# Attention and mixture of experts in one kernel: the attention's output projection in three 16-bit passes, and what is reordered around it

## The chip, the cores and the metric

The kernel runs on one core of a Trainium2 chip. The metric is the device time of one execution in microseconds (us). A core has TensorE (PE, with its own queue of weight loads, PEld), VectorE (DVE), ScalarE (ACT), GpSimd (POOL) and SyncE (SP), which here issues the transfers. Each engine runs its own list of instructions in order; they meet at semaphores.

## What is computed

x has 2048 tokens of 512 features. The first half is a recurrence over tokens, in 8 heads of 64, with a decay that depends on the data:

```
xn = layernorm(x) * gamma + beta
w  = sigmoid(xn @ Wx @ Ww + bw);  k = xn @ Wk;  v = xn @ Wv;  r = sigmoid(xn @ Wr)
state = (1 - w_t)[..., None] * state + k_t[..., None] * v_t[..., None, :]     (for each token t)
y_t   = r_t . state
x1 = layernorm(x + y @ Wo)
```

The second half is a mixture of 12 experts, two for each token, and another layernorm. The change touches only the first half. What matters is the product y @ Wo, in f32, for each group of 128 tokens.

## The kernel before, in words

**Chunks and pairs.** The 2048 tokens are 16 chunks of 128 (n = 0 to 15). Two chunks are a pair, and the projections of a pair (decay z, key k, receptance r, value v) are ten jobs on TensorE: jobs 0 and 1 transpose the normalised x (function `job`, L248), 2 and 3 make the decays, 4 and 5 the keys, 6 and 7 the receptances, 8 and 9 the values. They write the two banks of pA in turn, and ScalarE empties them (`take`, L590). The weights of these jobs are held as a high and a low f16 half, and x as xh and xl, so that each product is three f16 matmuls: high by high, high by low, low by high. xh is ScalarE's copy (L620), xl the rest, which VectorE subtracts (`low_x`, L814).

**A chunk on TensorE** (`chunk`, L369) is a list written by hand. scores(0) and scores(1) are the decayed products of keys and receptances for two halves of the heads (pS); between them VectorE copies what the masks select from pS to ST (`mask`, L818, eight instructions). apply_values(0) and (1) multiply ST by the values into pY. read_state adds what the state before gives, turn_keys transposes the decayed keys into pM, from where ScalarE copies them to kbT (L685). write_state makes the state's increment from kbT. attend_out(n − 1) (L341) is the output projection of the chunk before: yT, ScalarE's copy of pY (L724), by w_o, into pM. VectorE adds pM to x (`add_out`, L883) and takes statistics (`take_stats`).

While it does chunk n, TensorE also does jobs of the next pair. `fill(0)` to `fill(4)` are the five places for them. An odd chunk (FIRST) does jobs 0 and 1 and then 2, 3, 4, 5, one in each of the first four places; an even chunk (SECOND) does 6, 7, 8, 9. Chunk 0 is peeled, chunks 1 to 12 are three rounds of a hardware loop of four chunks, so that there are two turns back to the loop's start (after chunks 4 and 8), and chunks 13 to 15 are written out; in these the five places hold the gate's transposes and products, and ScalarE normalises finished tiles (`norms`).

**The levels.** The scores of chunk n + 1 need keys and receptances that are multiplied by products of decays, in seven levels, in the tiles L. VectorE does one half of the receptance levels (`dve_level`, L540, L546, L547, L555), ScalarE copies the other (L502), GpSimd does the keys' half (`pool_level`, L571) and ScalarE copies the rest (L515). The products of decays, AM, are VectorE's `dve_decays` (L525, seven instructions for a pair), at the start of an odd chunk. Besides this ScalarE and GpSimd split the experts' weights into f16 halves, three pieces a chunk (`act_piece` L523, `pool_piece` L577), which SyncE loads and stores.

**Order around the change.** The code sets all of it. TensorE, odd chunk: scores(0), read_state, turn_keys, jobs 0 and 1, projection, job 2, apply(0), scores(1), job 3, write_state, jobs 4 and 5, apply(1). ScalarE, odd chunk: normalise, key level 0, receptance level 1, key level 1, kbT, key level 2, takes 0 and 1, xh, key level 3, the state's decay, key level 4, receptance 2, key 5, receptance 3, a piece, receptance 4, take 2, receptance 5, a piece, take 3 and so on, and yT at the end. VectorE, odd chunk: decays, level 0, mask of scores(0), xl, levels 1 and 2, add_out, levels 3 to 6, mask of scores(1), state, statistics.

## Time and profile before

| What | Value |
|---|---|
| Three runs | 856.07, 857.55, 864.34 us; median 857.55 |
| The profiled execution, its own time | 859.21 us |
| Its span | 857.4 us |
| Mean granted clock of TensorE | 0.932 of full |
| Busy: PE, PEld, DVE, ACT, POOL | 725.9, 525.2, 498.7, 342.1, 328.7 us |

The attention half takes the span from 0 to about 500 us; its loop of chunks runs from about 89 to 410. The rest is the experts. Rows below name an instruction by its line (L349), its engine and operation, what it writes and reads, and how many were merged ("x8"). An f32 matmul is recorded as two. A bracket at the end is the idle time of the engine ahead of the row and what ended it.

### The profile page before, as it was taken

Reading aid. Unit: us, or ns where it says so; the run is one execution under the profiler, and the core shown is the slowest. Engines: PE = TensorE matmul, PEld = TensorE weight load, DVE = VectorE, ACT = ScalarE, POOL = GpSimd, SP = SyncE. Lnnn points to the kernel's source line nnn. Section 1 sums busy time; section 2 is a strip of 40 time slices with the busy share of each in tenths; the row PEclk is TensorE's granted clock in tenths of the full one; section 3 lists DMA queues with packets and bytes.
Section 4 is the critical chain, followed back from the end, with each engine's and each line's share of the span. In section 5 each row is a group of like instructions: output and inputs, shape, how many; then the busy total and the mean of one; then the engine's idle time right before and its main releaser. Section 6 shows DMA issues by size and latency. Waiting matters only on the chain. (4 is left out here: it accounts for less than half of the span.)

```text
span 857.4 us, 18313 instructions
## 1 busy us (share of the span) xinstructions
PE 725.9 (85%) x6030; PEld 525.2 (61%) x6031; DVE 498.7 (58%) x1035; ACT 342.1 (40%) x675; POOL 328.7 (38%) x355
## 2 busy tenths in 40 slices
PE   5879999998999989999969861799999999999400
PEld 2658787876877769778636521466666666666200
DVE  4655867666677646775756558244445444444285
ACT  4454645546345444554466220222222222222154
POOL 0345534542445425454244002243343434333262
PEclk9999999998999989999969975799999999999855
DMA  8615345431454324433342066144466557322394
GB/s 339 225 37 165 117 127 149 148 106 45 149 148 133 105 62 149 141 106 99 101 148 78 22 224 266 50 158 143 165 217 234 197 183 245 122 95 89 134 336 155
DMA packets 38867, 126.75 MB, mean 148 GB/s; under 512 B 3984, under 2 KB 4368, under 8 KB 36496
## 3 DMA queue, kind: packets, MB, share of 16 engines
q1 hardware_dynamic: 31920, 103.31, 35.7%
q0 software_dynamic: 6880, 22.55, 7.7%
q8 instruction: 42, 0.69, 0.3%
q14 instruction: 25, 0.20, 0.1%
HBM read 81.02 MB, written 44.83 MB: 147 GB/s over the span
## 5 line engine op out<-in xcount | busy, mean ns | idle before, releaser
L831 DVE COPY_PREDICATED ST<-msk,pS 128x256 f32<-128x256 uint8 x224 | 121.1, 569 | 100.1 <-issue 65.9
L577 POOL TENSOR_TENSOR piece_parts<-piece,piece_parts 128x1024 f16<-128x1024 f32 x48 | 104.6, 2179 | 115.5 <-ACT piece_parts L523 115.5
L571 POOL TENSOR_TENSOR L<-L,AM 128x256 f32<-128x256 f32 x96 | 70.9, 738 | 118.4 <-ACT L L515 108.8
L1236 PE MATMUL pH<-ring,xgh 128*128 x344 | 104.5, 304 | 5.3 <-issue 2.8
L1237 PE MATMUL pH<-ring,xgh 128*128 x344 | 104.1, 303 | 0.0
L1238 PE MATMUL pH<-ring,xgl 128*128 x344 | 104.1, 303 | 0.0
L299 PE MATMUL pS<-L 64*128 64x64 f32 x1536 | 99.2, 276 | 1.8 <-issue 1.7
L1552 POOL DMA_INDIRECT y_scratch<-ysb,sidx x43 | 42.9, 998 | 136.3 <-DVE ysb L1478 136.3
L299 PEld LDWEIGHTS pS<-L 64*128 64x128 f32 x1536 | 93.6, 192 | 2.1 <-issue 2.1
L1462 DVE TENSOR_TENSOR hid<-pH,sil 128x320 f32<-128x320 f32 x43 | 21.1, 492 | 119.6 <-ACT sil L1315 119.6
L555 DVE TENSOR_TENSOR L<-L,AM 128x256 f32<-128x256 f32 x96 | 70.6, 735 | 16.1 <-ACT L L502 10.0
L1315 ACT ACTIVATE sil<-pH 128x320 f32<-128x320 f32 x43 | 18.8, 437 | 131.0 <-PE pH L1238 131.0
L349 PE MATMUL pM<-w_o,yT 128*128 128x512 f32 x128 | 59.8, 611 | 4.3 <-ACT yT L724 2.8
L523 ACT CAST piece_parts<-piece 128x1024 f16<-128x1024 f32 x48 | 50.1, 1043 | 24.4 <-DMA piece<-in_w_experts 24.4
L1539 POOL DMA_INDIRECT xg<-x_scratch,gidx x43 | 42.7, 994 | 34.0 <-POOL gidx L1536 30.8
L1254 PE MATMUL pO<-ring,hTh 128*128 x129 | 49.0, 380 | 1.8 <-DVE hTh L1473 1.4
L1255 PE MATMUL pO<-ring,hTh 128*128 x129 | 48.9, 379 | 0.0
L1236 PEld LDWEIGHTS pH<-ring,xgh 128*128 128x128 f16 x344 | 34.0, 99 | 24.3 <-issue 11.1
L502 ACT COPY L<-L 128x256 f32<-128x256 f32 x80 | 32.5, 407 | 38.2 <-DVE L L555 26.9
L1311 ACT CAST hTh<-pHT 128x384 f16<-128x384 f32 x43 | 20.6, 479 | 63.9 <-PE pHT L1244 63.9
L1478 DVE COPY ysb<-pO 128x512 f32<-128x512 f32 x43 | 29.7, 692 | 23.0 <-PE pO L1255 23.0
L1237 PEld LDWEIGHTS pH<-ring,xgh 128*128 128x128 f16 x344 | 33.9, 99 | 13.4
(206 smaller groups left out, 1623.6 us busy)
## 6 DMA issues: line engine op xcount, KB each, us to landing
piece<-in_w_experts SPq DMA_DIRECT2D x48, 512.0 KB, 5.5
w_split_scratch<-piece_parts SPq DMA_DIRECT2D x48, 512.0 KB, 3.9
ring<-w_split_scratch SPq DMA_DIRECT2D x12, 2048.0 KB, 8.6
yin<-y_scratch SPq DMA_DIRECT2D x16, 512.0 KB, 5.8
x_scratch<-X SPq DMA_DIRECT2D x1, 4096.0 KB, 14.1
out_x<-X SPq DMA_DIRECT2D x8, 512.0 KB, 2.8
X<-in_x SPq DMA_DIRECT2D x1, 3072.0 KB, 23.3
X<-in_x SPq DMA_DIRECT2D x2, 512.0 KB, 7.5
```

The source lines that it names most:

```text
L299: i = pe.matmul(o, k_, r_, start=True, stop=True)
L349: i = pe.matmul(pM[:, 0, :], yT[:, g, :], w_o[:, g, :], start=(g == 0), stop=(g == KT - 1))
L523: a.copy(piece_parts[buf][:, 0, :], piece[buf][:, :]).then_inc(piece_hi, 1)
L555: v.tensor_tensor(next_grown(k, lv, 1), grown(rec, k, lv, 1), factor(c, lv, 0), ALU.mult).then_inc(r_dec, 1)
L571: g.tensor_tensor(next_kept(k, lv, 0), kept(key, k, lv, 0), by, ALU.mult).then_inc(k_dec, 1)
L577: g.tensor_tensor(piece_parts[buf][:, 1, :], piece[buf][:, :], piece_parts[buf][:, 0, :], ALU.subtract).then_inc(piece_lo, 1)
L831: v.copy_predicated(out[:, :, :, 0 if lv == 0 else 1, :], msk[:, lv, :, :].rearrange(shape, m=m), pS[:, :, lv * S:(lv + 1) * S].rearrange( ...
L1236: pe.matmul(p[:, 0, 0:F], xgh[par][:, k, :], wh, start=(k == 0), stop=False)
L1237: pe.matmul(p[:, 0, 0:F], xgh[par][:, k, :], wl, start=False, stop=False)
L1238: t = pe.matmul(p[:, 0, 0:F], xgl[par][:, k, :], wh, start=False, stop=(k == KT - 1))
L1254: pe.matmul(pO[:, 0, :], hTh[:, k, :], wh, start=(k == 0), stop=False)
L1255: t = pe.matmul(pO[:, 0, :], hTh[:, k, :], wl, start=False, stop=(k == FT - 1))
```

## The change

Wo is held as two f16 halves, wo_h and wo_l, and y as yTh (ScalarE's f16 copy of pY) and yTl (VectorE's subtraction, `low_y`). The projection is three f16 matmuls for each of the four blocks in place of one f32 matmul. Wo arrives in two transfers, in tiles that the second pair doesn't use yet (val[1] and rec[1]); before chunk 0 ScalarE makes wo_h in two copies, and GpSimd makes wo_l in two subtractions between its chunks 0 and 1. ScalarE's takes of jobs 6 and 8 of pair 1 wait until these tiles are read.

The order changes too. On TensorE, apply(1) goes ahead of the place `fill(3)`. In odd chunks jobs 0 and 1 go ahead of read_state, and job 2 goes from ahead of apply(0) to behind scores(1). read_state and the projection wait for y_low as well. On ScalarE, yTh is made behind `fill(2)`; in odd chunks the takes of jobs 0 and 1 go ahead of kbT, and xh and key level 2 follow it. On VectorE low_y comes ahead of level 0, the decays of a pair are made at the end of the even chunk, ahead of the loop's branch, and wait for the decay jobs only.

```diff
-        w_o = sb("w_o", [P, KT, C])
+        wo_h = sb("wo_h", [P, KT, C], F16)
+        wo_l = sb("wo_l", [P, KT, C], F16)
...
+        wo_stage = [val[1][:, :, :], rec[1][:, :, :]]
...
-            sp.dma_start(w_o[:, :, :], wo).then_inc(w_in[5], 16)
+            for i in range(2):
+                sp.dma_start(wo_stage[i], wo[:, 2 * i:2 * i + 2, :]).then_inc(w_in[5], 16)
...
                 pe.wait_ge(y_out, n + 1)
+                pe.wait_ge(y_low, n + 1)
...
             def attend_out(n):
+                pe.wait_ge(wo_lo, 2)
                 pe.wait_ge(y_out, n + 2)
+                pe.wait_ge(y_low, n + 2)
...
                 for g in range(KT):
-                    i = pe.matmul(pM[:, 0, :], yT[:, g, :], w_o[:, g, :], start=(g == 0), stop=(g == KT - 1))
+                    pe.matmul(pM[:, 0, :], yTh[:, g, :], wo_h[:, g, :], start=(g == 0), stop=False)
+                    pe.matmul(pM[:, 0, :], yTh[:, g, :], wo_l[:, g, :], start=False, stop=False)
+                    i = pe.matmul(pM[:, 0, :], yTl[:, g, :], wo_h[:, g, :], start=False, stop=(g == KT - 1))
...
                 scores(n, k, 0)
-                read_state(n, k)
-                turn_keys(n, k)
                 if slots is FIRST:
                     job(q, 0, par)
                     job(q, 1, par)
-                else:
+                read_state(n, k)
+                turn_keys(n, k)
+                if slots is not FIRST:
                     fill(0)
...
+                apply_values(n, k, 0)
+                scores(n, k, 1)
                 if slots is FIRST:
                     fill(0)
-                apply_values(n, k, 0)
-                scores(n, k, 1)
                 fill(1)
                 write_state(n, k)
                 fill(2)
+                apply_values(n, k, 1)
                 fill(3)
-                apply_values(n, k, 1)
                 fill(4)
...
-                    v.wait_ge(a_out, q * JOBS + 8)
+                    v.wait_ge(a_out, q * JOBS + (8 if isinstance(q, int) and q == 0 else 4))
...
             if lv == 0:
+                v.wait_ge(a_out, q * JOBS + 8)
...
+                if isinstance(q, int) and q == 1 and (m == 6 or m == 8):
+                    a.wait_ge(wo_lo, 2)
...
-                if m == 1:
-                    a.wait_ge(a_out, order(q, m) + 1)
-                    a.copy(xh[par][:, :, :], xf[:, :, :]).then_inc(x_hi, 1)
+            def high_x(q, par):
+
+                a.wait_ge(a_out, order(q, 1) + 1)
+                a.copy(xh[par][:, :, :], xf[:, :, :]).then_inc(x_hi, 1)
...
-                a.wait_ge(m_full, n * 3 + 1)
-                a.copy(kbT[:, :], pM[:, 0, :]).then_inc(kb_out, 1)
-                key_levels(2)
                 if slots is FIRST:
                     take(q, 0, par)
                     take(q, 1, par)
-                key_levels(3)
+                a.wait_ge(m_full, n * 3 + 1)
+                a.copy(kbT[:, :], pM[:, 0, :]).then_inc(kb_out, 1)
+                if slots is FIRST:
+                    high_x(q, par)
+                key_levels(2, 3)
...
                 fill(2)
+                a.wait_ge(st_used, n * 2 + 4)
+                a.copy(yTh[:, :, :], pY[:, 0, :].rearrange("p (g t) -> p g t", g=KT)).then_inc(y_out, 1)
                 norms(2)
                 fill(3)
                 norms(3)
-                a.wait_ge(st_used, n * 2 + 4)
-                a.copy(yT[:, :, :], pY[:, 0, :].rearrange("p (g t) -> p g t", g=KT)).then_inc(y_out, 1)
...
             a.wait_ge(stat1, 9)
+            for i in range(2):
+                a.wait_ge(w_in[5], 32)
+                a.copy(wo_h[:, 2 * i:2 * i + 2, :], wo_stage[i]).then_inc(wo_hi, 1)
             chunk(0, 0, 0, 0, (1, 1, SECOND))
...
-                if k % 2 and nxt is not None:
-                    dve_decays(v, n + 1, nxt, in_pair(k + 1)[0])
+                if not isinstance(n, int) or n:
+                    low_y(n - 1)
                 level(0)
...
                     take_stats(n - 1)
+                if k % 2 == 0 and (not isinstance(n, int) or n == 0):
+                    dve_decays(v, n + 2, nxt + 1, in_pair(k + 2)[0])
+
+            def low_y(n):
+
+                v.wait_ge(y_out, n + 2)
+                v.tensor_tensor(yTl[:, :, :], pY[:, 0, :].rearrange("p (g t) -> p g t", g=KT), yTh[:, :, :], ALU.subtract).then_inc(y_low, 1)
...
-            for n in range(2):
-                pool_chunk(g, n, n, 0)
+            pool_chunk(g, 0, 0, 0)
+            for i in range(2):
+                g.wait_ge(wo_hi, i + 1)
+                g.tensor_tensor(wo_l[:, 2 * i:2 * i + 2, :], wo_stage[i], wo_h[:, 2 * i:2 * i + 2, :], ALU.subtract).then_inc(wo_lo, 1)
+            pool_chunk(g, 1, 1, 0)
```

What this does to the lists, at three places. The line numbers of the changed kernel differ from those of the one before. First TensorE in the first odd chunk of the loop, from the end of scores(0); ISA and REGISTER_ALU are waits and counts. Before:

```order
L299 MATMUL pS<-L 128x64 x12
L304 REGISTER_ALU
L306 REGISTER_ALU
L309 MATMUL pY<-L,state 128x128 x4
L329 MATMUL pM<-idt,L 128x128 x4
L253 ISA
L256 ISA
L259 MATMUL pA<-idt,pair_x 128x128 x8
L349 MATMUL pM<-w_o,yT 128x512 x4
L253 REGISTER_ALU
L263 REGISTER_ALU
```

In the changed kernel:

```order
L306 MATMUL pS<-L 128x64 x12
L260 ISA
L263 ISA
L266 MATMUL pA<-idt,pair_x 128x128 x8
L311 REGISTER_ALU
L314 REGISTER_ALU
L317 MATMUL pY<-L,state 128x128 x4
L337 MATMUL pM<-idt,L 128x128 x4
L359 MATMUL pM<-wo_h,yTh 128x512
L360 MATMUL pM<-wo_l,yTh 128x512
L361 MATMUL pM<-wo_h,yTl 128x512
```

The jobs 0 and 1 (pA<-idt,pair_x) have moved ahead of read_state (pY<-L,state) and turn_keys (pM<-idt,L), which the projection now follows directly, in three f16 passes; behind it job 2 (L270, pA<-xh,wh_z) no longer stands.

Second ScalarE in the same chunk, from key level 1 on (L515 before, L526 after). Before:

```order
L515 COPY L<-L 128x128x2
L684 ISA
L685 COPY kbT<-pM 128x512
L507 REGISTER_ALU
L508 REGISTER_ALU
L515 COPY L<-L 128x64x4
L593 ISA
L601 ACTIVATE pair_x<-pA,vecs 128x256 x2
L593 REGISTER_ALU
L601 ACTIVATE pair_x<-pA,vecs 128x256 x2
L620 CAST xh<-pair_x 128x1024
```

In the changed kernel:

```order
L526 COPY L<-L 128x128x2
L605 ISA
L615 ACTIVATE pair_x<-pA,vecs 128x256 x2
L605 REGISTER_ALU
L615 ACTIVATE pair_x<-pA,vecs 128x256 x2
L703 ISA
L704 COPY kbT<-pM 128x512
L636 CAST xh<-pair_x 128x1024
L518 REGISTER_ALU
L519 REGISTER_ALU
L526 COPY L<-L 128x64x4
```

kbT has gone behind the two takes (pair_x<-pA,vecs), and the copy xh follows it, ahead of key level 2.

Third VectorE at the loop's turn, from the state on. Before:

```order
L867 ISA
L872 TENSOR_TENSOR state<-pM,sdec 64x4x64 x2
L880 ISA
L880 BN_STATS stats<-X 128x6
L936 REGISTER_ALU
L936 COMPARE_AND_BRANCH
L538 TENSOR_TENSOR AM<-dec 128x512
L538 TENSOR_TENSOR AM<-AM 128x256
```

In the changed kernel, from the decays' last products on:

```order
L546 REGISTER_ALU
L549 TENSOR_TENSOR AM<-AM 128x16
L546 REGISTER_ALU
L549 TENSOR_TENSOR dec_end<-AM 128x8
L967 REGISTER_ALU
L967 COMPARE_AND_BRANCH
L906 TENSOR_TENSOR yTl<-pY,yTh 128x512
L558 TENSOR_TENSOR L<-rec,dec 128x256
L559 TENSOR_TENSOR L<-rec,AM 128x256
```

The products of decays (AM<-AM) stand behind the branch before and ahead of it now, and low_y (yTl) is the first instruction behind it.

## Rows read from the trace of the kernel before

**Rows 1.** The page's 40 slices: TensorE busy, granted clock, in tenths.
```profile
PE   5879999998999989999969861799999999999400
...
PEclk9999999998999989999969975799999999999855
```

**Rows 2.** Waits of TensorE, 60 to 430 us: total, times, longest in us.
```profile
PE pA L270 <- DVE xl L816: 4.5, 6, 0.8
...
PE pS L299 <- ACT L L515: 2.9, 1, 2.9
```

**Rows 3.** TensorE's timeline, odd chunk: start, us, engine, line, operation, count, [idle before].
```profile
250.77 0.44 PE L299 MATMUL pS<-rec,key 64*128 64x64 f32 x4
...
254.49 1.16 PE L309 MATMUL pY<-L,state 128*128 128x128 f32 x8
...
256.85 3.67 PE L349 MATMUL pM<-w_o,yT 128*128 128x512 f32 x8
261.33 0.27 PE L270 MATMUL pA<-xh,wh_z 128*128 128x256 f16 x1 [0.81 <-DVE xl L816]
...
270.98 1.06 PE L337 MATMUL pM<-val,kbT 128*128 128x128 f32 x8
...
277.21 0.66 PE L319 MATMUL pY<-ST,val 128*64 128x128 f32 x8
```

**Rows 4.** Timeline of TensorE, chunk 13: projection and the instruction behind it.
```profile
419.27 3.67 PE L349 MATMUL pM<-w_o,yT 128*128 128x512 f32 x8 [0.77 <-ACT kbT L685]
422.87 0.66 PE L319 MATMUL pY<-ST,val 128*64 128x128 f32 x8
```

**Rows 5.** Timeline of TensorE, values job: first and thirteenth matmul.
```profile
407.33 0.38 PE L276 MATMUL pA<-wh_v,xh 128*128 128x512 f16 x1
...
409.92 0.38 PE L276 MATMUL pA<-wh_v,xh 128*128 128x512 f16 x1
```

**Rows 6.** Timeline of VectorE, the odd chunk of rows 3.
```profile
247.98 1.68 DVE L538 TENSOR_TENSOR AM<-dec 128x512 f32<-128x512 f32 x1
...
251.80 0.43 DVE L546 TENSOR_TENSOR L<-rec,dec 128x256 f32<-128x256 f32 x1
...
264.37 2.92 DVE L555 TENSOR_TENSOR L<-L,AM 128x256 f32<-128x256 f32 x2 [0.38 <-ACT L L502]
268.57 1.31 DVE L831 COPY_PREDICATED ST<-msk,pS 128x256 f32<-128x256 uint8 x2 [1.28 <-PE pS L299]
...
273.13 0.42 DVE L834 COPY ST<-pS 64x256 f32<-64x256 f32 x1
```

**Rows 7.** The same form on VectorE (L910): ns, min/median/max.
```profile
L910 DVE TENSOR_TENSOR wl_z<-pS,wh_z x4: 676/688/692, 18.0 to 28.3; 128x512 f16<-128x512 f32 x4
```

**Rows 8.** Timeline of ScalarE, the same odd chunk.
```profile
264.97 0.40 ACT L502 COPY L<-L 128x256 f32<-128x256 f32 x1
```

**Rows 9.** Timeline of GpSimd, the last piece ahead of its chunk 1.
```profile
67.07 2.14 POOL L577 TENSOR_TENSOR piece_parts<-piece,piece_parts 128x1024 f16<-128x1024 f32 x1 [2.63 <-ACT piece_parts L523]
```

**Rows 10.** Timeline of ScalarE, chunk 0.
```profile
71.79 0.59 ACT L685 COPY kbT<-pM 128x512 f32<-128x512 f32 x1 [1.32 <-PE pM L329]
```

**Rows 11.** Timeline of VectorE, chunk 0.
```profile
80.85 2.17 DVE L831 COPY_PREDICATED ST<-msk,pS 128x256 f32<-128x256 uint8 x3
```

**Rows 12.** Timeline of TensorE, chunk 0: apply(0) and apply(1).
```profile
75.40 0.66 PE L319 MATMUL pY<-ST,val 128*64 128x128 f32 x8 [1.03 <-DVE ST L834]
...
88.51 0.66 PE L319 MATMUL pY<-ST,val 128*64 128x128 f32 x8
```

**Rows 13.** Timeline of TensorE, end of the last chunk.
```profile
488.36 0.66 PE L319 MATMUL pY<-ST,val 128*64 128x128 f32 x8
491.85 5.24 PE L349 MATMUL pM<-w_o,yT 128*128 128x512 f32 x8 [2.83 <-ACT yT L724]
```

**Rows 14.** TensorE behind turn 2: length, busy, clock (1.00: 2.4 GHz), DMA.
```profile
306.00:314.00 8.00, 7.91 (x74) 0.58 0.11 39
```

**Rows 15.** Timeline of VectorE, the second loop turn.
```profile
305.23 0.69 DVE L538 TENSOR_TENSOR AM<-dec 128x512 f32<-128x512 f32 x1 [5.14 <-issue]
```

More of the change, by code:

```diff
@@ L116, in attention @@
         kbT = sb("kbT", [P, C])
-        yT = sb("yT", [P, KT, P])
+        yTh = sb("yTh", [P, KT, P], F16)
+        yTl = sb("yTl", [P, KT, P], F16)
         state = sb("state", [P, KT, P])
@@ L166, in attention @@
         y_out = sem("y_out")
+        y_low = sem("y_low")
+        wo_hi = sem("wo_hi")
+        wo_lo = sem("wo_lo")
         m_full = sem("m_full")
@@ L424, in _ @@
             pe.wait_ge(setup_done, 1)
-            pe.wait_ge(w_in[5], 16)
             chunk(0, 0, (1, 1, SECOND))
@@ L751, in _ @@
             take(0, 1, 0)
+            high_x(0, 0)
             high(0)
@@ L763, in _ @@
                 take(q, m, q)
+                if m == 1:
+                    high_x(q, q)
                 if at == 1:
@@ L894, in _ @@
             v.sem_inc(state_new, 1)
+            v.sem_inc(y_low, 1)
             v.sem_inc(x1_ready, 1)
@@ L942, in _ @@
                 chunk(n, n, None if n == NT - 1 else NPAIR - 1)
+            low_y(NT - 1)
             add_out(NT - 1)
```

## The prediction

> **What bounds the kernel now.** I read three views in this order: the page's slices, the waits, and then the timeline engine by engine over one odd and one even chunk. The slices show that TensorE is nearly full from about 60 to 410 us, and that after the loop (slice 20 and later) it is not [rows 1]. The waits of that stretch say the same from the other side: TensorE waits little there, 4.5 us for the low half of x (six times, once per odd chunk) and 2.9 us at one loop turn [rows 2]. So in the twelve looped chunks every microsecond of matmul counts, as long as VectorE delivers its masks in time. In the last three chunks and at the end other waits decide.
>
> The timeline of the odd chunk that starts at 250.77 is my measure [rows 3]: scores(0) to 254.49, then read_state, turn_keys and the two transposing jobs to 256.85, the output projection to about 260.45, a wait of 0.81 for the low half of x, job 2 from 261.33, apply(0) and scores(1), write_state at 270.98, apply(1) at 277.21. The next chunk starts at 277.8, so the odd chunk takes 27.0 us.
>
> **The change part by part.**
>
> *Projection in 16 bits.* Before: four f32 matmuls of 512 columns, from 419.27 to the next instruction at 422.87, 3.60 us [rows 4]. Now: twelve f16 matmuls of the same 512 columns. The trace has just that form in the values job: twelve of them start between 407.33 and 409.92, 2.59 us [rows 5]. The gain is 1.0 us for each projection at full clock.
>
> *Even chunks (six in the loop).* Nothing else on TensorE's path changes there but the place of apply(1), which now stands ahead of the last job. In the odd chunk shown the mask of scores(1) runs from 268.57 to 273.55 (273.13 + 0.42) [rows 6] while TensorE, without its last job of 2.65, would ask for it at 277.21 − 2.65 = 274.56 [rows 3]. An even chunk has the same jobs in these places (two jobs and write_state behind scores(1)), so some 1 us is left over. 6 × 1.0 = 6.0 us gained. The bounds are 0 (the mask becomes late by as much) and 6.0.
>
> *New VectorE work.* low_y is a subtraction of a 128x512 f16 copy from PSUM; the trace has that form, 688 ns [rows 7]. It stands ahead of level 0 and so ahead of the mask of the next scores(0). Before an odd chunk VectorE does the decays first: 247.98 to 251.87, 3.9 us [rows 6], then now 0.7 of low_y, then level 0 with some 0.8 to 1.4. That ends near 253.8 against the end of scores(0) at 254.49 [rows 3]: hidden, with 0.7 us to spare. If the cover went, each odd chunk would pay 0.7 or more. The waits for yTh ahead of it (ACT copies it right behind apply(1)) are covered by the last job and scores(0), 2.65 + 3.7 us. Moving the decays to the end of the even chunk changes their place only against the loop's branch and low_y.
>
> *Odd chunks: two waits change places.* The x matmuls of job 2 no longer follow the projection but scores(1), so the wait of 0.8 for the low half goes [rows 2, 3]. But the transposing jobs, which stood between turn_keys and the projection, now stand ahead of read_state, so that nothing covers the copy kbT. Chunk 13 has that order in the trace already: the projection waits 0.77 for kbT [rows 4]; with the latency I count 0.9. One wait pays for the other. Left is the 1.0 of the projection: TensorE would be at the end of job 2 at about 267.3.
>
> *Odd chunks: a new wait behind job 2.* ACT's list is unchanged there: the take of job 2 (L612) stands between the receptance copies of level 4 and level 5. Before, job 2 ended near 264.05 (261.33 and its 2.7) and, behind the take, the level 5 copy ran from 264.97 to 265.37, 1.3 us behind the job's end [rows 8]. Now job 2 ends at 267.3, so that copy ends at 268.6. VectorE's last level waits for it (level 6, the second in the row at 264.37 [rows 6], some 0.5), and only then the mask of scores(1) starts: 269.2. The mask takes 273.55 − 268.57 = 4.98 and ends at 274.2. TensorE meanwhile has done job 3, write_state and job 4 in the 6.2 us between 270.98 and 277.21 shifted [rows 3], 267.3 + 2.65 + 0.9 + 2.65 = 273.5, and wants apply(1): it waits 0.7. So the odd chunk ends at 274.2 + 0.6 + 2.65 = 277.5 instead of 277.8: 0.3 gained, 6 × 0.3 = 1.8 us. Bounds: 1.0 each if the mask is not late (6.0), and 0.5 lost each if it is 1.5 late instead of 0.7.
>
> *Chunk 0.* Wo must be split. ACT copies two 128x1024 pieces, and GpSimd subtracts two, between its chunks 0 and 1. The subtraction has the form of the expert pieces, 2.14 us for the one at 67.07, behind which chunk 1's first key level started at about 69.2 [rows 9]. Two of them push that level to about 73.5, 4.3 us later. ACT's level 1 key copy waits for it and kbT is queued behind. ACT had 1.32 us of idle time ahead of kbT [rows 10], so kbT comes 3.0 later; the levels that follow have about 0.6 of slack more. The mask of scores(1), at 80.85 before [rows 11], starts near 83.2 and ends near 88.2, while TensorE, which had apply(1) behind a last job at 88.51 [rows 12], now wants it at about 85.9. I charge 2.3 us. Bounds: 0 (the slack is larger) and 4.3 (all of it shows). The clock may add to it (below).
>
> *The last three chunks.* TensorE is no longer the bound there [rows 1]: ACT's normalising, VectorE's masks and the gate are. Full gain would be 3.0, none 0, and yTh now stands ahead of some of ACT's normalising and can push gate work by half a microsecond. I take 0.7.
>
> *The last projection.* Before, ACT normalised three tiles and then copied yT: apply(1) at 488.36, projection at 491.85 after an idle 2.83, and 5.24 long because the clock fell in that idle time [rows 13]. Now yTh follows apply(1) at once: 488.36 + 0.6 + 0.6, low_y 0.7 and a hop give 490.3; the twelve matmuls take 5.24 × 2.59 / 3.60 = 3.8. End 494.1 instead of 497.1: 3.0 gained. Bounds 1.5 (same start, less work) and 4.2 (full clock).
>
> Sum: 6.0 + 1.8 − 2.3 + 0.7 + 3.0 = 9.2 us. The experts' part is not touched. The profiled execution took 859.2 (span 857.4), so it would take 850.0; the median shown is 857.55, and 9.2 less is 848.3. A change of 1% (8.6 us) is about what a measurement can tell from no change; the forecast lies just beyond it.
>
> **The clock.** Behind the loop turn at which TensorE had waited 2.9 us, the granted clock was 0.58 in the mean of the 8 us from 306 to 314 [rows 2, 14]: mostly the lower level, 1.2 GHz. That costs a full TensorE 8 × 0.42 = 3.4 us. It did not fall behind the wait of 1.03 in chunk 0 [rows 12] nor behind the 0.8s. The new wait of 2.3 lies between these cases.
>
> **The rivals.**
>
> 1. *The mask is not late in the odd chunks* (0.22). For it: all my terms there are tenths, and VectorE has idle time ahead of that mask (1.28 [rows 6]). Against it: ACT's list. Gain 4.2 more: 844.1.
>
> 2. *The clock falls in chunk 0* (0.20). For it: a wait of 2.3 us. Against: the wait of 1.03 had no such effect. 3.4 more: 851.7.
>
> 3. *VectorE comes late as well at loop turns or at level 0* (0.09). VectorE has a gap of 5.14 us at a turn [rows 15]. It lay ahead of the decays; it will lie between the decays and low_y, for which read_state now waits: the decays to 303.9, a gap of 5.1, low_y 0.7 and level 0 0.8 end at 310.5, against scores(0), which in the slow clock ended near 311.8. Hidden by 1.3 us by these rows; where it is not, or where level 0 meets GpSimd in the other odd chunks, a microsecond for each odd chunk gives 854.5.
>
> The Trainium skill (Runtime: NRT & Kernel Launch, section on instruction fetch mechanics) says that a taken branch to code that isn't in the engine's small window of instructions stops the engine until that page is fetched. By that rule the gap belongs to the branch and not to the decays, so it moves with the branch and can't be hidden by moving the decays; the trace agrees so far as there is such a gap at the turn.
>
> 4. *Slower: the clock falls in every odd chunk* (0.07). Mechanism: each odd chunk now has two waits, 0.9 ahead of the projection and 0.7 ahead of apply(1), in place of one. If these together are enough to bring the clock to half, each costs 3.4 us: 848.3 + 6 × 3.4 = 868.7. [...]
>
> 5. *The gain doesn't show* (0.06): the masks, not the matmuls, set the pace in even chunks too, so only the end gains: 857.55 − 3.0 + 2.3 = 856.9.
>
> The forecast itself has 0.36.
>
> **How the numbers follow.** Time: that of the forecast, 848.3. Faster by over 1% means under 849.0: rival 1 whole (0.22), about six tenths of the forecast's own spread (0.22), and 0.04 for the clock staying up at a turn or at the end: 0.48. Slower by over 1% means above 866.1: rival 4 and a little for what I don't see, 0.08. Within 1%: the rest, 0.44. The range goes from 841 (rival 1 with a better end and one turn without a fall of the clock) to 857 (rival 5), which leaves out rival 4 and thin ends.
>
> **What would show it.** Right: twelve projection matmuls in 2.6 us; TensorE's waits hold kbT ahead of the projection six times with 0.8 to 0.9, VectorE's last copy of ST ahead of apply(1) about six times with 0.7, once with 2.3 in chunk 0, and no wait for xl; the last projection starts within 2.2 us of apply(1). Wrong: a mask of scores(1) in an odd chunk that starts as soon as scores(1) ends (rival 1); a granted clock of 0.50 at about 90 us (rival 2) or in each odd chunk (rival 4); waits of read_state for yTl (rival 3); even chunks that don't shrink from their old length by 1.0 (rival 5).

## The result

The changed kernel took 854.68 us (median of 20 executions, 849.57 to 861.52) against 859.97 of before in the same session (20, 853.37 to 864.34): a ratio of 0.9945, with a 95% interval of 0.9918 to 0.9971. So it is faster by about 0.55%, 4.7 us, where 9.2 us was forecast. (The 4.7 goes by the ratio; the two medians alone lie 5.3 apart.) Two later series of the same kernel, which stand below, gave 0.9922 and 0.9931.

The profiled execution took 860.72 us (span 858.9), which is near the upper end. Against [rows 1] the granted clock lost a tenth in slices 10 and 38 and two in slice 23, and gained one in slice 24; busy time lost one in slices 5, 10, 20 and 22 and gained one in slice 23. A tenth of a slice is only 2 us, so these rows show where to look and not how much.

```profile
PE   5879899997999989999868961799999999999400
...
PEclk9999999997999989999969785799999999999755
```

TensorE's waits from 60 to 430 us, the answer to [rows 2] (total, times, longest in us):

```profile
PE pY L327 <- DVE ST L857: 6.0, 8, 2.3
PE pM L359 <- ACT kbT L704: 5.6, 7, 0.8
PE pS L306 <- issue: 3.5, 2, 2.0
PE pS L306 <- ACT L L526: 2.7, 1, 2.7
```

The wait for xl is gone. kbT stands in its place (0.77 to 0.82 in each odd chunk of the loop, forecast 0.9), the mask ahead of apply(1) is new (0.43 to 0.45 in each, forecast 0.7), and chunk 0 waits 2.29 (forecast 2.3). Here are those three in TensorE's timeline, with the projection of an odd chunk between: from its first matmul at 151.81 to apply(0) at 154.49 it takes 2.68, against 3.60 before [rows 4].

```profile
88.98 0.66 PE L327 MATMUL pY<-ST,val 128*64 128x128 f32 x8 [2.29 <-DVE ST L857]
...
151.81 0.38 PE L359 MATMUL pM<-wo_h,yTh 128*128 128x512 f16 x1 [0.82 <-ACT kbT L704]
...
154.49 0.66 PE L327 MATMUL pY<-ST,val 128*64 128x128 f32 x8
...
168.16 0.66 PE L327 MATMUL pY<-ST,val 128*64 128x128 f32 x8 [0.43 <-DVE ST L857]
```

**Where the time went.** I lay the two profiled executions beside each other by the starts of apply(0). The table's forecast is the sum's own.

| Stretch | Measured, us | Forecast, us |
|---|---|---|
| to apply(0) of chunk 0 (75.40, now 76.10) | +0.7 | 0 |
| chunk 0 with chunk 1 (52.02, now 54.95) | +2.9 | +1.0 |
| three pairs without a turn (52.02, now 50.90, 50.88 and 50.89) | −3.4 | −3.9 |
| pair with turn 1 (57.65, now 58.09) | +0.4 | −1.3 |
| pair with turn 2 (58.38, now 56.91) | −1.5 | −1.3 |
| the last three chunks (12 to 13, 13 to 14, 14 to 15) | −0.6, +1.4, +5.7 | −0.7 |
| the end, up to the experts' first matmul | −3.7 | −3.0 |
| sum, up to the experts (500.48, now 502.50) | +2.0 | −9.2 |

The experts' part is as long as it was (356.9, now 356.4). The one large entry is 14 to 15: 22.48 before, 28.21 now. TensorE's timeline there:

```profile
466.84 0.66 PE L327 MATMUL pY<-ST,val 128*64 128x128 f32 x8 [0.62 <-DVE ST L857]
467.43 0.66 PE L374 MATMUL pA<-idt,X 128*128 128x128 f32 x4
469.30 1.09 PE L374 MATMUL pA<-idt,X 128*128 128x128 f32 x4 [1.21 <-ACT logitT L660]
470.31 0.69 PE L306 MATMUL pS<-rec,key 64*128 64x64 f32 x4
470.80 0.63 PE L306 MATMUL pS<-rec,L 64*128 64x64 f32 x4
471.23 2.77 PE L306 MATMUL pS<-L 64*128 64x64 f32 x24
```

The waits are small, 0.62 and 1.21. But the 24 score matmuls behind them take 2.77 where such a row takes 1.50 at full clock, and L374 with four matmuls takes 1.09 instead of 0.66. The clock was at its lower level, 1.2 GHz, from about 468 to 484, which costs 6.8 us (from the granted clock in steps of 2 us). Two stretches as windows (length, then busy time and count of PE, PEld, DVE, ACT and POOL, granted clock, DMA share, GB/s), chunk 0 and this one:

```profile
86.00:95.00 9.00, 6.71 (x42) 3.03 (x41) 8.10 (x16) 2.96 (x5) 3.58 (x4) 0.81 0.63 191
...
455.00:485.00 30.00, 28.02 (x218) 20.47 (x216) 16.79 (x31) 12.76 (x26) 8.10 (x6) 0.77 0.24 72
```

So the waits are where they were forecast, and near the forecast in size; the clock behind them is not in the forecast's sum. What of this belongs to the change and what to one execution is what the first and the last run ask.

### The profile page after: what moved, and what is told of

It reads as the page before. It is cut to its first block and busy times, and to the rows that moved or that the text cites. A ratio compares the mean times of both kernels' runs of the same rounds, so it can differ in the third digit from the quotient of the medians.

```text
span 858.9 us, 18498 instructions
## 1 busy us (share of the span) xinstructions
PE 720.7 (84%) x6094; PEld 524.8 (61%) x6095; DVE 506.8 (59%) x1051; ACT 344.7 (40%) x677; POOL 334.3 (39%) x357
## 5 line engine op out<-in xcount | busy, mean ns | idle before, releaser
L583 POOL TENSOR_TENSOR L<-L,AM 128x256 f32<-128x256 f32 x96 | 73.6, 767 | 120.4 <-ACT L L526 114.7
L306 PE MATMUL pS<-L 64*128 64x64 f32 x1536 | 102.3, 281 | 2.0 <-issue 2.0
L306 PEld LDWEIGHTS pS<-L 64*128 64x128 f32 x1536 | 96.8, 198 | 2.3 <-issue 2.2
L1273 PEld LDWEIGHTS pH<-ring,xgl 128*128 128x128 f16 x344 | 34.0, 99 | 12.0
```

The source lines that it names most:

```text
L306: i = pe.matmul(o, k_, r_, start=True, stop=True)
L583: g.tensor_tensor(next_kept(k, lv, 0), kept(key, k, lv, 0), by, ALU.mult).then_inc(k_dec, 1)
L1273: t = pe.matmul(p[:, 0, 0:F], xgl[par][:, k, :], wh, start=False, stop=(k == KT - 1))
```

## The experiments

The runs came in three series on three chips, with before in each. The first (before at 858.52 us, 15 executions) has the same kernel again, the three passes, kbT's cover and Wo. The second (858.64, 28) has the order alone, job 2's take, the tail and all four edits. The third (858.42, 16) has the last three runs. Ratios are to before of the same series, with their 95% intervals. The diffs are against the changed kernel unless it is said otherwise, and show its main places; "..." stands for lines between them. None leaves work out.

**The same kernel again.** No edit.

> The changed kernel itself, once more, to see which stretches at half clock recur. Theory A (each new wait that follows from the order of the lists costs its own length, and the clock fall near 90 us belongs to the wait of 2.3 us in chunk 0): the waits are the same to 0.1 us (kbT 0.8 six times, ST 0.45 six times and 2.3 once), the clock is again below 0.9 in 90 to 100 us; the fall at 470 to 480 us need not come back. Rival B (where the clock falls is chance): the waits are the same, but the fall near 90 is gone too. Either way the time is 0.4 to 0.8% under the kernel before.

850.52 us (6 executions, 849.38 to 858.9), ratio 0.9922 (0.9879 to 0.9965). The profiled execution took 850.04, with the same waits, and the clock in chunk 0 was again 0.81. Behind chunk 14 it did not fall, although both waits there were a little longer than above, 0.66 and 1.50:

```profile
86.00:95.00 9.00, 6.70 (x49) 3.52 (x50) 8.25 (x17) 3.48 (x6) 3.06 (x3) 0.81 0.62 200
455.00:485.00 30.00, 27.38 (x287) 19.75 (x286) 19.45 (x37) 12.01 (x24) 7.88 (x5) 1.00 0.24 72
```

14 to 15 took 22.75 here, against 28.21. The experts started at 494.99, 5.5 us ahead of before. So the fall behind chunk 14 differs from execution to execution with the program unchanged. The one in chunk 0 came back here, but it does not come always either: two kernels below have the same chunk 0 and the same wait, and no fall.

**The three passes in before's order.**

```diff
                 scores(n, k, 0)
+                read_state(n, k)
+                turn_keys(n, k)
                 if slots is FIRST:
                     job(q, 0, par)
                     job(q, 1, par)
-                read_state(n, k)
-                turn_keys(n, k)
-                if slots is not FIRST:
+                else:
                     fill(0)
...
+                if slots is FIRST:
+                    fill(0)
                 apply_values(n, k, 0)
                 scores(n, k, 1)
-                if slots is FIRST:
-                    fill(0)
...
                 fill(2)
+                fill(3)
                 apply_values(n, k, 1)
-                fill(3)
```

The decays and ScalarE's list go back to their places too.

> The three 16-bit passes in the order of the kernel before (jobs 0 and 1 behind turn_keys, job 2 ahead of apply(0), apply(1) and yTh last, decays behind the branch). Theory A: even chunks keep their gain (6 x 0.75 = 4.5 us); in odd chunks the projection ends 0.9 sooner but job 2 then waits for xl, which hangs on the mask of scores(0): the six waits of 0.8 grow to about 1.7 and the odd chunks gain nothing; chunk 0 loses 0.3 instead of 2.3; the end gains 1 instead of 3. Total near -6, about as good as the changed kernel. Rival C (the reordering is what gains, the passes alone gain nothing): even chunks still take 25.0 us and the time is that of the kernel before.

859.22 us (10 executions), 1.0005 (0.9983 to 1.0028): no gain, where some 6 us was expected. Waits of TensorE, 60 to 430:

```profile
PE pA L277 <- DVE xl L839: 8.8, 6, 1.7
...
PE pY L317 <- DVE yTl L906: 2.5, 1, 2.5
PE pY L327 <- DVE ST L857: 1.2, 2, 1.1
```

The odd chunk stays at 26.97: of the 0.9 that the projection saves, the wait for xl takes all (0.8 becomes 1.7 at the longest). xl is VectorE's, and it comes no sooner because TensorE is. The even chunk does gain (−0.85), 5.1 us in six. Most of that was lost again at two places of this profile: 3.7 us from chunk 0 to 1, where read_state of chunk 1 waits 2.5 for yTl and the clock falls behind it (1.7), and 3.1 us behind chunk 14 (25.53 against 22.48), also at the lower clock. In chunk 0 VectorE's copies to ST end at 88.2, against 85.8 before, so Wo's set-up delays this kernel there too. The wait for xl takes the odd chunks' gain; the set-up and the clock take most of the rest.

**The order alone, with before's f32 projection.** Against before:

```diff
                 scores(n, k, 0)
-                read_state(n, k)
-                turn_keys(n, k)
                 if slots is FIRST:
                     job(q, 0, par)
                     job(q, 1, par)
-                else:
+                read_state(n, k)
+                turn_keys(n, k)
+                if slots is not FIRST:
                     fill(0)
```

and the other moves of the change on TensorE, ScalarE and VectorE.

> The kernel before, with its f32 projection and Wo whole, in the changed kernel's order (jobs 0 and 1 ahead of read_state, job 2 behind scores(1), apply(1) and yT early, decays ahead of the branch). Theory A (the order alone gains nothing in the loop, it only makes room for the shorter projection): odd chunks pay 0.9 for kbT and 0.45 for the mask and save 0.8 of xl, about 0.5 longer than 27.0; even chunks stay at 25.0; the last projection starts 1.5 to 2 us sooner; in all 0 to +3 us. Rival C (the order is what gains): 3 us or more under the kernel before.

861.47 us (10), 1.0024 (0.9997 to 1.005). A pair takes 52.66, 0.64 more than before: the wait for kbT (0.8, seven times) stands in place of the one for xl, and the mask is late in odd chunks too. So each half of the change shows no gain by itself, and together they are worth the 4.7 us. In the odd chunks the shorter projection pays only where no wait behind it grows by what it saves.

**kbT gets its cover back.** Jobs 0 and 1 go behind turn_keys again, and ScalarE's kbT ahead of their takes; all else stays.

```diff
                 scores(n, k, 0)
+                read_state(n, k)
+                turn_keys(n, k)
                 if slots is FIRST:
                     job(q, 0, par)
                     job(q, 1, par)
-                read_state(n, k)
-                turn_keys(n, k)
-                if slots is not FIRST:
+                else:
                     fill(0)
...
                 key_levels(1)
+                a.wait_ge(m_full, n * 3 + 1)
+                a.copy(kbT[:, :], pM[:, 0, :]).then_inc(kb_out, 1)
+                key_levels(2)
                 if slots is FIRST:
                     take(q, 0, par)
                     take(q, 1, par)
-                a.wait_ge(m_full, n * 3 + 1)
-                a.copy(kbT[:, :], pM[:, 0, :]).then_inc(kb_out, 1)
-                if slots is FIRST:
                     high_x(q, par)
-                key_levels(2, 3)
+                key_levels(3)
```

> The changed kernel with jobs 0 and 1 back behind turn_keys (and ScalarE's kbT and key level 2 ahead of their takes); job 2 stays behind scores(1). Theory A: the six waits of 0.8 for kbT go; apply(0) is then held by the mask of scores(0) for about 0.3, so each odd chunk is about 0.55 shorter, 26.1 us instead of 26.6, 3.3 us in all; no wait for xl comes back. Rival: VectorE's low_x or the later takes become late instead and the odd chunk stays at 26.6.

847.86 us (5), 0.9863 (0.9828 to 0.9899). A pair takes 50.22, 0.68 less than in the changed kernel, which is 4.1 us in six pairs. (The time alone would not show it: the changed kernel of the same series has 0.9879 to 0.9965, and the two intervals overlap.) The wait for kbT is left once. Part of it turned up as more waits for the mask:

```profile
PE pY L327 <- DVE ST L857: 6.9, 12, 2.5
...
PE pM L359 <- ACT kbT L701: 0.8, 1, 0.8
```

**Job 2's take behind the last receptance level.**

```diff
                 rec_levels(4)
+                rec_levels(5)
                 if slots is FIRST:
                     fill(0)
-                rec_levels(5)
```

> The changed kernel with ScalarE's take of job 2 behind receptance level 5 instead of ahead of it. Theory A (that take, which waits for job 2, holds back VectorE's last level and so the mask of scores(1)): the six waits of 0.45 for ST ahead of apply(1) in odd chunks go, and a chunk pair takes 50.45 us instead of 50.90. Rival: VectorE's own work, low_y and the decays among it, makes the mask late; the waits stay at 0.45.

851.13 us (10), 0.9896 (0.9865 to 0.9927). This tests the step "a new wait behind job 2" and its rival 1. In the changed kernel scores(1) end at 158.9, but VectorE's last level waits for ScalarE's copy until 162.79, and the mask follows it at 163.14, 4.3 us behind scores(1) (first fence). Here scores(1) end at 157.6 and the mask starts at 159.38, 1.8 us behind them (second).

```profile
162.79 0.43 DVE L567 TENSOR_TENSOR L<-L,AM 128x256 f32<-128x256 f32 x1 [2.74 <-ACT L L513]
163.14 4.52 DVE L854 COPY_PREDICATED ST<-msk,pS 128x256 f32<-128x256 uint8 x7
```

```profile
156.55 2.91 DVE L567 TENSOR_TENSOR L<-L,AM 128x256 f32<-128x256 f32 x2 [0.42 <-ACT L L513]
159.38 1.29 DVE L854 COPY_PREDICATED ST<-msk,pS 128x256 f32<-128x256 uint8 x2
```

The six waits of 0.45 are gone (three are left in all, 3.5 us), and a pair takes 50.50. It was ScalarE's list, as forecast. The time itself is not clear of the changed kernel's (0.9918 to 0.9971): the 0.4 us of each pair, 2.4 in all, is seen in the profile. TensorE's wait of 2.30 in chunk 0 is in this profile as well; what the clock did behind it stands with the next edit.

**Wo split in idle time.** ScalarE copies wo_h earlier, in a wait for an expert piece, and VectorE subtracts in place of GpSimd.

```diff
+                    if at - 5 == PIECE_AT[2]:
+                        for i in range(2):
+                            a.wait_ge(w_in[5], 32)
+                            a.copy(wo_h[:, 2 * i:2 * i + 2, :], wo_stage[i]).then_inc(wo_hi, 1)
                     if at - 5 in PIECE_AT:
...
-            for i in range(2):
-                a.wait_ge(w_in[5], 32)
-                a.copy(wo_h[:, 2 * i:2 * i + 2, :], wo_stage[i]).then_inc(wo_hi, 1)
             chunk(0, 0, 0, 0, (1, 1, SECOND))
...
                 level(0)
+                if isinstance(n, int) and n == 0:
+                    for i in range(2):
+                        v.wait_ge(wo_hi, i + 1)
+                        v.tensor_tensor(wo_l[:, 2 * i:2 * i + 2, :], wo_stage[i], wo_h[:, 2 * i:2 * i + 2, :], ALU.subtract).then_inc(wo_lo, 1)
...
             pool_chunk(g, 0, 0, 0)
-            for i in range(2):
-                g.wait_ge(wo_hi, i + 1)
-                g.tensor_tensor(wo_l[:, 2 * i:2 * i + 2, :], wo_stage[i], wo_h[:, 2 * i:2 * i + 2, :], ALU.subtract).then_inc(wo_lo, 1)
```

> The changed kernel with Wo split in idle time: ScalarE's two copies ahead of its piece copy that waits for a transfer (3.8 us idle), the two subtractions on VectorE ahead of the first mask (6.4 us idle), none on GpSimd. Theory A: the wait of 2.3 us for ST ahead of apply(1) in chunk 0 goes (what is left is under 0.5), GpSimd's chunk 1 starts 4.3 us sooner, and the half clock near 90 us with it: 4 us gained against the changed kernel. Rival B (the clock falls there for another reason): 2.3 us gained and still a clock below 0.9 between 85 and 100 us.

848.57 us (4), 0.9872 (0.9836 to 0.9908), an interval that also overlaps the changed kernel's of the same series; what the edit does is read from the profile. In the changed kernel GpSimd stands like this. The two subtractions put the key level 4.2 us back, as forecast from [rows 9] (74.03 against 69.16 before, of which 0.7 was there ahead of them):

```profile
69.85 2.14 POOL L997 TENSOR_TENSOR wo_l<-val,wo_h 128x1024 f16<-128x1024 f32 x1
71.94 2.14 POOL L997 TENSOR_TENSOR wo_l<-rec,wo_h 128x1024 f16<-128x1024 f32 x1
74.03 0.85 POOL L583 TENSOR_TENSOR L<-key,dec 128x256 f32<-128x256 f32 x1
```

Without that, the key level starts at 69.14, apply(1) of chunk 0 waits for nothing, and the clock stays up:

```profile
85.85 0.66 PE L327 MATMUL pY<-ST,val 128*64 128x128 f32 x8
```

```profile
86.00:95.00 9.00, 9.00 (x103) 7.16 (x102) 8.49 (x15) 6.30 (x12) 4.39 (x4) 1.00 0.66 198
```

From apply(0) of chunk 0 to that of chunk 1 it is 23.57 against 27.49: 3.9 less, of which 2.3 is the wait and 1.7 the clock.

But the wait does not always bring the fall. The tail's edit (next) and that of job 2's take leave chunk 0 as the changed kernel has it. Their profiles have the same wait, 2.32 and 2.30, and the clock stays at its full level behind it (first row the tail's edit, second the take's):

```profile
86.00:95.00 9.00, 6.68 (x65) 3.98 (x62) 8.03 (x15) 3.98 (x7) 4.38 (x4) 1.00 0.66 196
86.00:95.00 9.00, 6.70 (x63) 3.96 (x63) 8.02 (x15) 3.93 (x7) 4.31 (x4) 1.00 0.69 199
```

There the same stretch takes 25.97 and 25.94. So of six profiles with this chunk 0 (three of the changed kernel, kbT's cover with a wait of 2.54, and these two) four had the fall and two had none, and the edit is worth 2.4 or 3.9 us. Rival 2 was right about the place, in four profiles of six, and twice too large in its size.

**The old order in chunks 13 and 14.** apply(1) and the copy to yTh go back behind `fill(3)` there.

```diff
-                apply_values(n, k, 1)
-                fill(3)
+                if isinstance(n, int) and n in (NT - 3, NT - 2):
+                    fill(3)
+                    apply_values(n, k, 1)
+                else:
+                    apply_values(n, k, 1)
+                    fill(3)
```

> The changed kernel, but in chunks 13 and 14 apply(1) stands behind fill(3) again and yTh behind the normalising, as before. Theory D (new: the changed kernel has two kinds of executions, near 850 and near 858, and what parts them is a stretch at half clock from about 468 to 484 us, behind two waits of 0.6 and 1.2 us at the end of chunk 14): the wait of 0.6 for ST goes, chunk 14 to 15 takes 22.7 us in the profile, no half clock near 470, and nearly all executions are near 850. Rival (the fall there is chance, whatever the waits): executions still lie in two groups, and the median stays at 854.

853.62 us (11), 0.9936 (0.9906 to 0.9966), which is not different from the changed kernel. The wait for the mask went, the gate's grew to 2.00, and the clock fell all the same (0.89 in the mean from 455 to 485, which cost 3.4 us; 14 to 15 took 25.67):

```profile
464.98 0.63 PE L374 MATMUL pA<-idt,X 128*128 128x128 f32 x4 [2.00 <-ACT logitT L664]
```

The theory that the early apply(1) is what makes the clock fall there is not borne out.

**All four edits.** kbT's cover, the take, Wo and the old order in 13 and 14.

> All four edits in one: Wo split in idle time, jobs 0 and 1 behind turn_keys, the take of job 2 behind receptance level 5, the old order in chunks 13 and 14. Theory A: the savings add, as each takes away a wait of TensorE of its own: 4 us in chunk 0, 4.0 in the odd chunks by kbT, up to 2.7 by the mask, and no second group of executions: 840 to 843 us, 1.9% under the kernel before. Rival: with kbT covered, the masks bound the odd chunks, and the saving of the take is not seen: 843 to 846.

847.63 us (6), 0.9846 (0.9807 to 0.9884), some 5 us above what was expected and above its rival too. A pair takes 49.7, as the parts would give, but the clock fell behind a gate wait of 2.0 in chunk 14: 14 to 15 took 27.26.

**Three edits: without the one in 13 and 14.**

> Three of the four edits: Wo split in idle time, jobs 0 and 1 behind turn_keys, the take of job 2 behind receptance level 5; chunks 13 to 15 as in the changed kernel. Theory D2 (the old order in chunk 14, not the merging of edits, made the clock fall in every execution of 'four', behind the gate's wait of 2.0 us): the loop's pairs take 49.7 us as there, chunk 13 to 14 takes 34.5 to 35.4, and executions lie in two groups, most near 841 to 844 (chunk 14 to 15 in 22.5 us), some 5 to 7 us above. Rival: all executions show the fall and lie near 848.

841.92 us (6, 840.58 to 849.7), 0.9824 (0.9777 to 0.9871). This is the best kernel of the study, 1.8% faster than before, and its interval lies wholly below those of all three series of the changed kernel. One of its six executions took 849.7, at a mean granted clock of 0.919 where the other five had 0.926 to 0.930. Its waits from 60 to 415:

```profile
PE pS L306 <- issue: 7.4, 4, 2.1
PE pY L327 <- DVE ST L858: 1.4, 3, 1.0
PE pM L359 <- ACT kbT L701: 0.8, 1, 0.8
```

Chunk 0 to 1 takes 22.77, an undisturbed pair 49.7 (52.02 before), and 14 to 15 22.54, with a mask wait of 0.66 and a gate wait of 1.30.

**Three edits and the old order in chunk 13 alone.**

> As 'three', and in chunk 13 alone apply(1) behind fill(3) and yTh behind the normalising. Theory D2: chunk 13 to 14 takes about 33 us instead of 34.5 to 35.4 (no wait of 3.6 to 4.2 for ST ahead of apply(1) there), chunk 14 is as in the changed kernel, so the lower group is near 840 to 842. Rival: what is saved in chunk 13 is spent in a fall of the clock at chunk 14, and it is no faster than 'three'.

845.78 us (6), 0.9858 (0.9818 to 0.9898). 13 to 14 hardly shrank (34.3 to 34.14, where 33 was expected), and the clock fell behind chunk 14, behind waits of 0.64 and 1.10: 14 to 15 took 26.95.

**The changed kernel a third time.** No edit.

> The changed kernel a third time, beside these on one chip. Theory D: executions in two groups, about 850 to 852 and 856 to 861, and the profile shows chunk 14 to 15 in about 22.7 us if its time is in the lower group and about 28 if in the upper; the fall of the clock near 90 us and the other waits are there in either. Rival: the length of chunk 14 to 15 doesn't go with the time.

851.0 us (9, 848.86 to 862.14), 0.9931 (0.9894 to 0.9968); profiled 850.03, 14 to 15 in 22.57 with the clock at full level, mask wait 0.64, gate wait 1.35.

The changed kernel has 35 executions in all (20, 6 and 9), from 848.9 to 862.1 us. The two groups that were expected are not there: the times between 852 and 857 are filled. But the spread goes with the clock. Each execution's mean granted clock is on record: the 10 that took 856.2 us or more had 0.919 to 0.924, the 16 below 852.5 had 0.927 to 0.933, and over all 35 the correlation of the time with what was lost to the clock (the span times one minus the mean clock) is 0.94, at 0.9 us of time for each us lost. Of the three that were profiled, the one with the fall behind chunk 14 is at 860.7, and the two without it are at 850.0. So most of the spread is the clock's; which stretches make it up is known for the profiled executions only.

## Why the prediction was right and wrong

**The waits: right.** Even chunks 0.74 shorter (forecast 1.0), odd ones 0.4 (forecast 0.3). kbT for xl was the exchange that the sum had, the take of job 2 was what made the mask late (rival 1 fell), and 2.3 in chunk 0 came out to the tenth. The miss in the pairs (1.12 for 1.3, 1.1 us over six pairs) has several small parts. The projection was priced 2.59 from thirteen starts in one job [rows 5] and takes 2.68 to the next instruction, as the last step, to an instruction of another form, is 0.31 us where the others are 0.22. That is 0.09 in each chunk. Each falls short by nearly 0.2 more, which was not traced, and the odd one gets back 0.3 to 0.4 from shorter waits for kbT and the mask. The end gained 3.7 for 3.0: the last projection took 2.6 us at full clock, where I had put 3.8 with the clock low as before. Rivals 4 and 5 fell with the waits: away from the turns the clock stayed at its full level through the loop's odd chunks, and the even ones did shrink.

**Rival 3: no.** read_state never waited for yTl in the changed kernel. At turn 1 VectorE has its gap between the decays and low_y (first fence), where before it was ahead of the decays (second, and [rows 15] for turn 2):

```profile
197.37 0.17 DVE L549 TENSOR_TENSOR dec_end<-AM 128x8 f32<-128x8 f32 x1
201.91 0.69 DVE L906 TENSOR_TENSOR yTl<-pY,yTh 128x512 f16<-128x512 f32 x1 [4.37 <-issue]
```

```profile
194.38 0.69 DVE L538 TENSOR_TENSOR AM<-dec 128x512 f32<-128x512 f32 x1 [3.96 <-issue]
```

The gap stayed with the branch. The Trainium skill (Runtime: NRT & Kernel Launch, section on instruction fetch mechanics) has the rule that a taken branch to a target outside the engine's window of two pages leads to a fetch; by that rule such a gap moves with the branch, and this trace agrees (the gap is 4.37 us). Turn 1 got no shorter all the same: in three profiles of three the time at the lower clock behind it cost 5.1 us, against 3.4 in the one profile of before. That is not the change's alone either, since the Wo edit and the tail's, which leave this turn as it is, had 3.4 there. At turn 2 the pair gained 1.5 in the first profile and 2.6 and 2.8 in the other two, for a forecast of 1.3, with the same 3.4 lost to the clock as before; this was not traced, and it is luck for the sum. (Rival 3's own figure has a slip: 848.3 and six times 1.0 make 854.3, not 854.5.)

**The failed step: the clock, which the sum put at nothing.** The prediction has "The clock may add to it (below)" and "The new wait of 2.3 lies between these cases". I then gave the clock to rival 2, for chunk 0 alone, and left it out of the 9.2. Measured in steps of 2 us from 60 to 485 us, the lower clock cost 13.7 us before, and 23.9, 17.1 and 15.4 in the three profiles of the changed kernel: 10.2, 3.4 and 1.7 us more. Of this 1.7 lies in chunk 0 each time, where the forecast's wait stood (with the same chunk 0 two other kernels had nothing), 1.7 behind turn 1 each time, and 6.8 behind chunk 14 in the first profile; the third had 1.7 less than before around 430. The gains up to the experts were −2.0, 5.5 and 7.5 us in these profiles; with the clock's extra added back they are 8.2, 8.9 and 9.2, near the forecast's 9.2. This is an estimate, since a us of lower clock need not be a whole us of time. The executions that were not profiled point the same way: the mean of what was lost to the clock is 62.5 us over the 35 of the changed kernel and 59.7 over the 59 of before in the later series, 2.8 more (0.8 and 2.5 within the two series that have both), against 4.5 that the forecast misses.

**The mis-sized term: "The last three chunks … I take 0.7".** I bounded this between 3.0 and nothing, and let what could be lost there be half a microsecond of pushed gate work. In the profile first shown these chunks cost 6.5: 13 to 14 is 1.4 longer (in the other two 0.9 longer and 0.9 shorter), and 14 to 15 5.7 longer in that execution and 0.1 to 0.3 longer in the others. In those two the term is a loss of 0.6 and a gain of 1.3, so 0.7 was fair for them. The bound missed that short waits there can be followed by 16 us at 1.2 GHz.

**Left open.** What tips the clock isn't settled, neither in chunk 0 nor behind chunk 14. In chunk 0 the four profiles with the fall have their first apply(0) at 75.4 to 76.1 us and the two without it at 76.7 and 76.8, but no run here moves that start on purpose. The two waits of chunk 14 ended in a fall with 0.62 and 1.21 (the changed kernel's first profile) and with 0.64 and 1.10 (the last edit of the tail), and in none with 0.66 and 1.50, 0.64 and 1.35, and 0.66 and 1.30. Behind chunk 14, over the twelve profiles beside before's: of the eight with both waits (0.62 to 0.66 and 1.10 to 1.50) three had the fall, with kbT's cover the third, and of the four with the gate's alone all four (1.50, 1.97, 2.00 and 2.00), whereas before had 1.23 alone and none. So the length of the two short waits does not decide. Too few profiles of each kernel are there for how often it falls in each. Nor is it shown what the extra 1.7 at turn 1 hangs on, or the spread of the first apply(0), which lay between 75.3 and 76.8 over all thirteen profiles, of kernels that differ little before it.

## What to carry to other kernels

A shorter operation is worth what is left after the next wait on another engine has grown: list the next wait behind each place where it stands, and ask whether its releaser gets earlier too. Here the passes alone and the order alone each gave nothing that the times show, and together with an eye to kbT, the take and the set-up of Wo they gave 1.8%. Set-up work goes where an engine is idle, not where its turn happens to come: two subtractions of 2.14 us on GpSimd cost TensorE 2.3 us, and 3.9 where the clock fell behind the wait. And a new wait of about 1 to 2.5 us on a full TensorE has two prices, its own length and the time at the lower clock that may follow. The second can be the larger (6.8 us behind waits of 0.62 and 1.21), so it belongs in the sum with a chance, not in a rival only. Last, one profile of a kernel can't tell what the clock does: profile it more than once, and compare the mean granted clocks of all executions.

## What was not expected of the hardware

One wait of 2.3 to 2.5 us, with TensorE full before and after it, was followed by the lower clock at a cost of 1.7 us in four profiles and by nothing in two, with the same instructions in that chunk. Waits of 0.8 and 1.03 were never followed by it, nor were the ones for xl, up to 1.7, in the loop of the passes alone. Behind chunk 14, where a wait of 0.6 is followed 1.3 us later by one of 1.2 to 1.5, the changed kernel showed both outcomes, and the difference in 14 to 15 is 5.5 us. Its 35 executions spread over 13 us (848.9 to 862.1), and most of that goes with the mean granted clock.
